# Transposing x1 by DMA instead of by TensorE, and v's product in two other banks, in a pipeline of four normalised graph layers

## The chip, the cores and the metric

The kernel runs on one core of a Trainium2 chip. The metric is the device time in microseconds (us) of one execution, taken as the median over runs.

## The reference

Eight batches (B = 8) of 1024 nodes with 128 features pass through four layers that share one 1024x1024 adjacency matrix. After each layer the result is added to its input and normalised over the features:

```python
x = _layernorm(x + _L0_gnn_ref(x, adj, ...), axis=-1)   # y = (adj @ x + x) @ w + b, rows divided by their norm
x = _layernorm(x + _L1_gnn_ref(x, adj, ...), axis=-1)   # attention, below
x = _layernorm(x + _L2_gnn_ref(x, adj, ...), axis=-1)   # (si + sj + adj * w_r + g_b) @ x @ w + b
x = _layernorm(x + _L3_gnn_ref(x, adj, ...), axis=-1)   # relu of three Chebyshev terms of the Laplacian
```

Here x1 is the result of the first line. The second layer, which the change touches, is

```python
Q = x @ q
K = x @ k
A = jnp.einsum('bnd,bmd->bnm', Q, K) / jnp.sqrt(jnp.float32(128))
A = jnp.tanh(A / 8.0) * 8.0
A = jnp.exp(A) * A_shape
A = A / jnp.sum(A, axis=-1, keepdims=True)
out = A @ x @ v
```

## The kernel before

Every float32 operand of a matrix product is split into two float16 parts, hi and lo. ScalarE (ACT in the profile) writes hi, VectorE (DVE) then writes lo as the operand minus hi, and TensorE (PE) makes each product as three matmuls (hi by hi, hi by lo, lo by hi; `split_product`, L1230 to L1234). Nodes lie in C = 8 chunks of 128 on the partitions. For a product over features x1 is needed with the features on the partitions, which is x1T.

The instructions of each engine are written out by hand in one order, with semaphores between the engines. Nothing reorders them: an instruction that waits holds up all that stand behind it on its engine. One iteration i of the loop has a `front(i)` and a `back(i)`:

- `front(i)` is the attention of batch i. For each of eight chunks t, PE makes the scores (`scores`, `next_scores`) in r1 or r0 of PSUM, ACT takes tanh and exp of them (L389, L391), DVE multiplies by the adjacency (`mask`, L846), ACT writes p_hi (L279), DVE p_lo (L851), and PE adds the chunk into av (`attend`, L1370 to L1373). Between them PE does parts of layer 2 of batch i-1 (`adj_x2_part`, `sum_x2`, `sums_w2`), whose sums DVE reads from bank m7 (`sums_read`, L738) ahead of its first mask.
- `back(i)` finishes layer 2 of batch i-1, does layer 3 of batch i-1 (`laplacian_part`, products of xq with a_hi and a_lo into r0, which DVE reads in two halves in `end_sum`, L804, semaphore `fa`), and layer 0 of batch i+1. Last it prepares the attention of batch i+1: x1 is normalised (`norm` on ACT, `ln_norm` on DVE), transposed by PE (`x1_t`, L1238, float32, eight 128x128 blocks into r1), read back and split (`x1t_hi`, `x1t_lo`), and multiplied for g (`g_product`, into r2, that is banks 0 and 1 of av) and v (`v_product`, into r1). g and v are split in turn (`g_hi`, `g_lo`, `v_hi`, `v_lo`); `v_scaled` makes a third copy of v on ACT.

The order at this seam, before: PE does `x1_t`, the second part of the first half of the last Laplacian (48 matmuls), `g_product`, `v_product`, the second part of its second half (48 matmuls), and then `scores(i+1, 0)` after a wait for `v_lo`, since r1 holds v until DVE has read it, and `scores(i+1, 1)` after a wait for `fa`, since r0 holds the Laplacian until `end_sum(i-1, 1)` has read it. DVE does the steps of `sj_step` (sums of x2 with the gate's weights) around `x1t_lo`, then `end_sum(i-1, 0)`, `g_lo`, `v_lo`, `x0_max(i+2)` (L608, absent in the last round), `end_sum(i-1, 1)`, `sj_step` 3, `sums_read`.

The sync engine (SP) issues all transfers. In the loop it loads x[i+1] when layer 0 has used x0, and stores the result of batch i-2.

```python
                x1t_lo(i + 1, r1)
                sj_step(sj_ch, i, 2)
                end_sum(i - 1, 0)
                g_lo(i + 1, r2)
                v_lo(i + 1, r1)
                if i + 2 < B:
                    x0_max(i + 2)
                end_sum(i - 1, 1)
                sj_step(sj_ch, i, 3)
```

Of the kernel before, what the change touches and what calls it, by code (L numbers as in the profile page):

```python
# [13 lines left out]
P = 128  # L14
# [62 lines left out]
def adj_resnorm(nc, x, adj, adj_t, w_first, w2, w3, rows, out):  # L77
    ctx = ExitStack()
    with ctx:
# [33 lines left out]
        x1T = sb("x1T", [P, 2, N], F16)  # L113
        xts = (x1T, sb("x1Tb", [P, 2, N], F16))
# [80 lines left out]
        def _(sp):  # L195
# [17 lines left out]
            for i in range(2, B):  # L213
                if i < B - 1:
                    sp.wait_ge(S["e0"], i + 1)
                    sp.dma_start(x0[:], x[i + 1]).then_inc(S["x_in"], 16)
                sp.wait_ge(S["ln3_a"], i - 1)
                sp.dma_start(out_v[i - 2], outb[:]).then_inc(S["stored"], 16)
# [58 lines left out]
        def _(act):  # L277
# [90 lines left out]

            def g_hi(b, src):
                for h in range(2):  # L370
                    act.wait_ge(S["g_mm"], 2 * b + h + 1)
                    copy(gs[b % 2][:, 0, half(h)], src[:, half(h)], W_DOWN).then_inc(S["g_hi"], 1)

            def v_hi(b, src):
                for h in range(2):
                    act.wait_ge(S["v_mm"], 2 * b + h + 1)
                    copy(vhis[b % 2][:, half_chunks(h), 0:D], cd(src[:])[:, half_chunks(h)], W_DOWN).then_inc(S["v_hi"], 1)
# [29 lines left out]
            def start():  # L407
# [15 lines left out]
                v_hi(0, r1)  # L423
# [11 lines left out]
                v_hi(1, r0)  # L435
# [22 lines left out]
            def back(i):  # L458
# [29 lines left out]
                x1t_hi(i + 1, r1)  # L488
                g_hi(i + 1, r2)
                v_hi(i + 1, r1)  # L490
# [44 lines left out]
        def _(dve):  # L535
# [377 lines left out]
            def start():  # L913
# [26 lines left out]
                v_lo(0, r1)  # L940
# [29 lines left out]
                v_lo(1, r0)  # L970
# [76 lines left out]
            def back(i, l2_ch):  # L1047
# [161 lines left out]
        def _(pe):  # L1209
# [167 lines left out]
            def start():  # L1377
# [14 lines left out]
                v_product(0, r1)  # L1392
# [21 lines left out]
                v_product(1, r0)  # L1414
# [33 lines left out]
            def front(i):  # L1448
# [50 lines left out]
            def back(i):  # L1499
# [133 lines left out]
```

## Time and profile before

| | |
|---|---|
| median of 3 runs | 692.7 us (691.31 to 693.2) |
| the profiled execution, its own time | 691.86 us |
| its span | 689.7 us |
| PE busy | 640.5 us, 93% |
| DVE busy | 587.4 us, 85% |
| ACT busy | 415.6 us, 60% |
| granted clock of PE, mean | 0.977 |
| hardware DMA queue, share of 16 engines | 7.7% |

The span is the profiled stretch from the first to the last instruction; the time of the same execution is 2.2 us longer. Busy time counts an engine as busy while a matmul is in its pipeline, so PE rows overlap: a 128-column matmul shows 0.22 us, and the next starts 0.056 us later. What a row of matmuls costs is therefore read from the distance of starts. The loop repeats from about 182 us to 565 us, five times, and each of these stretches takes 76.7 us.

### The profile page before, as it was taken

Reading aid. Unit: us, or ns where it says so; the run is one execution under the profiler, and the core shown is the slowest. Engines: PE = TensorE matmul, PEld = TensorE weight load, DVE = VectorE, ACT = ScalarE, POOL = GpSimd, SP = SyncE. Lnnn points to the kernel's source line nnn. Section 1 sums busy time; section 2 is a strip of 40 time slices with the busy share of each in tenths; the row PEclk is TensorE's granted clock in tenths of the full one; section 3 lists DMA queues with packets and bytes.
Section 4 is the critical chain, followed back from the end, with each engine's and each line's share of the span. In section 5 each row is a group of like instructions: output and inputs, shape, how many; then the busy total and the mean of one; then the engine's idle time right before and its main releaser. Section 6 shows DMA issues by size and latency. Waiting matters only on the chain. (4 is left out here: it accounts for less than half of the span.)

```text
span 689.7 us, 17526 instructions
## 1 busy us (share of the span) xinstructions
PE 640.5 (93%) x7435; PEld 478.3 (69%) x7435; DVE 587.4 (85%) x1521; ACT 415.6 (60%) x719; POOL 73.0 (11%) x49
## 2 busy tenths in 40 slices
PE   8897768799999999999999999999999999789895
PEld 3454536469766996669766986679666986448794
DVE  7878879688998898998998898989998889789535
ACT  6969578425692659646692649555792659323512
POOL 0102100002001100012001100021001100111002
PEclk9999988999999999999999999999999999989998
DMA  9610000000000020002000020002000000000102
GB/s 337 243 50 1 1 0 2 0 2 33 2 1 1 2 64 1 1 1 64 1 2 1 2 63 1 2 1 64 1 1 1 24 11 1 1 1 3 31 3 62
DMA packets 12446, 18.75 MB, mean 27 GB/s; under 512 B 592, under 2 KB 9040, under 8 KB 12368
## 3 DMA queue, kind: packets, MB, share of 16 engines
q1 hardware_dynamic: 12368, 17.63, 7.7%
q8 instruction: 58, 0.95, 0.6%
q14 instruction: 20, 0.16, 0.1%
HBM read 13.44 MB, written 4.19 MB: 26 GB/s over the span
## 5 line engine op out<-in xcount | busy, mean ns | idle before, releaser
L238 POOL TENSOR_TENSOR small<-small,minus_half 128x8 f32<-128x8 f32 x39 | 68.6, 1763 | 590.4 <-DVE small L572 307.1
L846 DVE TENSOR_TENSOR att<-att,adjT 128x1024 f32<-128x1024 f32 x64 | 78.0, 1219 | 11.9 <-ACT att L391 11.8
L389 ACT ACTIVATE att<-r,coef 128x1024 f32<-128x1024 f32 x64 | 70.4, 1100 | 15.1 <-PE r L1234 14.4
L851 DVE SCALAR_TENSOR_TENSOR p_lo<-p_hi,att 128x1024 f16<-128x1024 f16 x64 | 77.9, 1219 | 0.0
L1234 PE MATMUL r<-xq,a_lo 128*128 128x128 f16 x448 | 76.0, 219 | 0.0
L1232 PE MATMUL r<-xq,a_hi 128*128 128x128 f16 x448 | 76.0, 219 | 0.0
L1233 PE MATMUL r<-xq,a_hi 128*128 128x128 f16 x448 | 76.0, 219 | 0.0
L1232 PE MATMUL r<-rs,a_hi 128*128 128x128 f16 x448 | 75.8, 219 | 0.0
L1234 PE MATMUL r<-rs,a_lo 128*128 128x128 f16 x448 | 75.8, 219 | 0.0
L1233 PE MATMUL r<-rs,a_hi 128*128 128x128 f16 x448 | 75.8, 219 | 0.0
L279 ACT ACTIVATE p_hi<-att 128x1024 f16<-128x1024 f32 x64 | 66.8, 1044 | 12.7 <-DVE att L846 12.7
L391 ACT ACTIVATE att<-att 128x1024 f32<-128x1024 f32 x64 | 67.7, 1057 | 2.0
L1370 PE MATMUL av<-vhib,p_hi 128*128 128x129 f16 x256 | 46.7, 226 | 10.1 <-DVE p_lo L851 9.9
L1370 PE MATMUL av<-vhi,p_hi 128*128 128x129 f16 x256 | 45.6, 223 | 8.8 <-DVE p_lo L851 8.6
L279 ACT ACTIVATE yT<-r 128x512 f16<-128x512 f32 x16 | 9.5, 596 | 65.2 <-PE r L1234 65.1
L1373 PE MATMUL av<-vhsb,p_lo 128*128 128x129 f16 x256 | 46.8, 226 | 0.0
L1372 PE MATMUL av<-vlob,p_hi 128*128 128x128 f16 x256 | 46.7, 225 | 0.0
L1373 PE MATMUL av<-vhs,p_lo 128*128 128x129 f16 x256 | 45.7, 223 | 0.0
L1372 PE MATMUL av<-vlo,p_hi 128*128 128x128 f16 x256 | 45.6, 222 | 0.0
L1233 PEld LDWEIGHTS r<-xq,a_hi 128*128 128x128 f16 x448 | 43.7, 98 | 0.1
L1234 PEld LDWEIGHTS r<-rs,a_lo 128*128 128x128 f16 x448 | 43.8, 98 | 0.0
L1232 PEld LDWEIGHTS r<-rs,a_hi 128*128 128x128 f16 x448 | 43.7, 98 | 0.0
(383 smaller groups left out, 2104.3 us busy)
## 6 DMA issues: line engine op xcount, KB each, us to landing
adjT<-in_adj_t SPq DMA_DIRECT2D x8, 512.0 KB, 8.1
x<-in_x SPq DMA_DIRECT2D x7, 512.0 KB, 4.8
out<-outb SPq DMA_DIRECT2D x7, 512.0 KB, 3.5
pq<-in_adj SPq DMA_DIRECT2D x2, 512.0 KB, 8.7
u<-in_adj SPq DMA_DIRECT2D x2, 512.0 KB, 9.3
tmp<-in_adj SPq DMA_DIRECT2D x2, 512.0 KB, 9.8
x2s<-in_adj SPq DMA_DIRECT2D x2, 512.0 KB, 9.5
outb<-in_x SPq DMA_DIRECT2D x1, 512.0 KB, 11.6
```

Of the source, the lines that this page charges most:

```text
L238: return nc.gpsimd.tensor_tensor(dst, src, minus_half[:], ALU.pow)
L279: return nc.scalar.activation(dst, src, ACT.Copy, scale=scale, **more)
L389: nc.scalar.activation(att[:, s], dst[:], ACT.Tanh, scale=c_tanh).then_inc(S["th"], 1)
L391: nc.scalar.activation(att[:, s], att[:, s], ACT.Exp, scale=TANH_CAP).then_inc(S["ex"], 1)
L846: tt(att[:, s], att[:, s], adjT[:, t, :], ALU.mult).then_inc(S["pm"], 1)
L851: stt(p_lo[:, s], p_hi[:, s], -LO_UP, att[:, s], ALU.mult, ALU.add).then_inc(S["pl"], 1)
L1232: mm(dst, s_hi, m_hi, start=start, stop=False, skip_group_check=True)
L1233: mm(dst, s_hi, m_lo, start=False, stop=False, skip_group_check=True)
L1234: return mm(dst, s_lo, m_hi, start=False, stop=stop, skip_group_check=True)
L1370: mm(acc, p_hi[:, s, chunk(j)], vhi[:, t, 0:D + 1], start=(t == 0 and j % 3 == 0), stop=False, skip_group_check=True)
L1372: mm(acc[:, 0:D], p_hi[:, s, chunk(j)], vlo[:, t, :], start=False, stop=False, skip_group_check=True)
L1373: l_ = mm(acc, p_lo[:, s, chunk(j)], vhs[:, t, 0:D + 1], start=False, stop=(t == C - 1), skip_group_check=True)
```

## The change

Twelve transfers with transposition (two for each of the batches 2 to 7) take the place of six calls of `x1_t`. ACT and DVE split x1 as it lies in rows (`x1_row_hi`, `x1_row_lo`, both from SBUF) into a new buffer x1r, SP issues a transfer for hi when hi is written and one for lo when lo is written, and `g_product` waits for both to have landed. For batches 0 and 1 nothing changes but the way in which the banks of v are named.

On PE the first half of the last Laplacian now comes directly after the first parts, then half of what was the last block (24 matmuls), `g_product`, the other 24, and `v_product` at the very end. v goes to `av[:, 2]` and m7. `scores(i, 0)` waits for `g_lo`, and the wait for `v_lo` stands behind `scores(i, 1)`, ahead of the first write to m7. On DVE `x1_row_lo` stands ahead of the first three steps of `sj_step`.

```diff
@@ SP @@
+            for i in range(1, B - 1):
+                if i + 2 < B:
+                    sp.wait_ge(S["e0"], i + 2)
+                    sp.dma_start(x0[:], x[i + 2]).then_inc(S["x_in"], 16)
+                if i >= 2:
+                    sp.wait_ge(S["ln3_a"], i - 1)
+                    sp.dma_start(out_v[i - 2], outb[:]).then_inc(S["stored"], 16)
+                for part, name in enumerate(("hi", "lo")):
+                    sp.wait_ge(S[f"x1r_{name}"], i)
+                    sp.dma_start(cd(xts[(i + 1) % 2][:, part]), x1r[:, part], transpose=True).then_inc(S[f"x1d_{name}"], 16)
...
@@ ACT @@
+            def x1_row_hi(b):
+                act.wait_ge(S["ln0_v"], b + 1)
+                act.wait_ge(S["ln0_a"], b + 1)
+                if b > 2:
+                    act.wait_ge(S["x1d_hi"], 16 * (b - 2))
+                copy(cd(x1r[:, 0]), xas[b % 2][:], X_UP).then_inc(S["x1r_hi"], 1)
...
-                x1t_hi(i + 1, r1)
+                x1_row_hi(i + 1)
                 g_hi(i + 1, r2)
-                v_hi(i + 1, r1)
+                v_hi(i + 1, (av[:, 2], m7))
                 v_scaled(i + 1)
@@ DVE @@
+            def x1_row_lo(b):
+                if b > 2:
+                    dve.wait_ge(S["x1d_lo"], 16 * (b - 2))
+                dve.wait_ge(S["x1r_hi"], b - 1)
+                stt(cd(x1r[:, 1]), xas[b % 2][:], X_UP, cd(x1r[:, 0]), ALU.mult, ALU.subtract).then_inc(S["x1r_lo"], 1)
...
                 q_lo(z_all, i - 1, 1)
-                for k_ in range(2):
+                x1_row_lo(i + 1)
+                for k_ in range(3):
                     sj_step(sj_ch, i, k_)
-                x1t_lo(i + 1, r1)
-                sj_step(sj_ch, i, 2)
                 end_sum(i - 1, 0)
                 g_lo(i + 1, r2)
-                v_lo(i + 1, r1)
+                v_lo(i + 1, (av[:, 2], m7))
@@ PE @@
             def g_product(b, dst):
                 xt = xts[b % 2]
+                if b >= 2:
+                    pe.wait_ge(S["x1d_hi"], 16 * (b - 1))
+                    pe.wait_ge(S["x1d_lo"], 16 * (b - 1))
                 for h in range(2):
-                    pe.wait_ge(S["x1t_lo"], 2 * b + h + 1)
+                    if b < 2:
+                        pe.wait_ge(S["x1t_lo"], 2 * b + h + 1)
...
-                pe.wait_ge(S["v_lo"], 2 * (i + 1))
+                pe.wait_ge(S["g_lo"], 2 * (i + 1))
                 scores(i, 0)
                 pe.wait_ge(S["fa"], 2 * (i - 1))
                 scores(i, 1)
+                pe.wait_ge(S["v_lo"], 2 * (i + 1))
...
                 laplacian_part(r0, xq, 1, 0, C // 2)
-                x1_t(i + 1, r1)
                 pe.wait_ge(S["q_lo"], 2 * i)
                 laplacian_part(r0, xq, 0, C // 2, C).then_inc(S["o_mm"], 1)
+                laplacian_part(r0, xq, 1, C // 2, 6)
                 pe.wait_ge(S["u_ok"], i)
                 g_product(i + 1, r2)
-                v_product(i + 1, r1)
-                laplacian_part(r0, xq, 1, C // 2, C).then_inc(S["o_mm"], 1)
+                laplacian_part(r0, xq, 1, 6, C).then_inc(S["o_mm"], 1)
+                v_product(i + 1, (av[:, 2], m7))
```

How the instructions stand on DVE at the end of `back(5)`, which prepares batch 6; before:

```order
L827 TENSOR_TENSOR tmp<-xb,bias 128x1024 [waits ln1_v,ln1_a]
L829 TENSOR_REDUCE sj<-tmp 128x8 [waits sj_c]
L830 CAST one_sj<-sj 128x8 [waits sj_c]
L730 SCALAR_TENSOR_TENSOR x1T<-r,x1T 128x512 [waits x1t_hi] x2
L832 TENSOR_TENSOR tmp<-xb,bias 128x1024
L833 TENSOR_TENSOR one_sj<-sj,one_sj 128x8 [waits sj_c]
L804 SCALAR_TENSOR_TENSOR u<-r,coef,u 128x512 [waits o_mm]
L730 SCALAR_TENSOR_TENSOR g<-av,g 128x512 [waits g_hi] x2
L730 SCALAR_TENSOR_TENSOR vlo<-r,vhi 128x512 [waits v_hi] x2
L608 TENSOR_REDUCE xmax<-x 128x1 [waits x_in]
L804 SCALAR_TENSOR_TENSOR u<-r,coef,u 128x512 [waits o_mm]
```

and with the change, from the same place:

```order
L881 SCALAR_TENSOR_TENSOR x1r<-xa,x1r 128x1024 [waits x1r_hi,x1d_lo]
L844 TENSOR_TENSOR tmp<-xb,bias 128x1024 [waits ln1_v,ln1_a]
L846 TENSOR_REDUCE sj<-tmp 128x8 [waits sj_c]
L847 CAST one_sj<-sj 128x8 [waits sj_c]
L849 TENSOR_TENSOR tmp<-xb,bias 128x1024
L850 TENSOR_TENSOR one_sj<-sj,one_sj 128x8 [waits sj_c]
L821 SCALAR_TENSOR_TENSOR u<-r,coef,u 128x512 [waits o_mm]
L747 SCALAR_TENSOR_TENSOR g<-av,g 128x512 [waits g_hi] x2
L747 SCALAR_TENSOR_TENSOR vlo<-av,vhi 128x512 [waits v_hi]
L747 SCALAR_TENSOR_TENSOR vlo<-m,vhi 128x512 [waits v_hi]
L625 TENSOR_REDUCE xmax<-x 128x1 [waits x_in]
L821 SCALAR_TENSOR_TENSOR u<-r,coef,u 128x512 [waits o_mm]
```

The two halves of x1T's lo (one row, x2) have become one instruction from SBUF at the head; v_lo, x0_max (xmax) and the second end_sum (u, the last row) stand in the same order as before, behind a product that PE now makes later.

On SP, the issues of the last rounds of the loop with the change; before, only the loads of x and the stores of out stood there:

```order
L220 DMA x<-in_x 128x1024 [waits e0]
L223 DMA out<-outb 128x8x128 [waits ln3_a]
L226 DMA_TRANSPOSE x1T<-x1r 128x8x128 [waits x1r_hi]
L226 DMA_TRANSPOSE x1T<-x1r 128x8x128 [waits x1r_lo]
L223 DMA out<-outb 128x8x128 [waits ln3_a]
```

The transposing transfers stand behind the load and the store of their round, and each waits for its half of the split.

## Rows read from the trace of the kernel before

**Rows 1.** The page: its first line.
```profile
span 689.7 us, 17526 instructions
```
**Rows 2.** Busy time in one period; columns: PE, PEld, DVE, ACT, POOL, clock, DMA.
```profile
411.80:488.50 76.70, 76.66 (x928) 58.44 (x926) 69.75 (x179) 49.19 (x89) 8.23 (x5) 1.00 0.05 15
```
**Rows 3.** PE alone: x1_t, 48 Laplacian matmuls, g_product, v_product; length and busy time.
```profile
479.62:480.50 0.88, 0.88 (x11) 1.00 0.00 0
480.50:483.18 2.68, 2.68 (x50) 1.00 0.03 6
483.18:484.48 1.30, 1.30 (x10) 1.00 0.00 0
484.48:485.82 1.34, 1.34 (x26) 1.00 0.00 0
```
**Rows 4.** Timeline of DVE at the seam: start, length, line, operation, count, idle before.
```profile
475.90 1.22 DVE L841 SCALAR_TENSOR_TENSOR x2s<-xb,x2s 128x1024 f16<-128x1024 f32 x1
...
478.62 1.14 DVE L797 SCALAR_TENSOR_TENSOR xq<-pq,q_scale,xq 128x128 f16<-128x128 f32 x4
479.67 1.23 DVE L827 TENSOR_TENSOR tmp<-xb,bias 128x1024 f32<-128x1024 f32 x1
...
484.79 0.75 DVE L804 SCALAR_TENSOR_TENSOR u<-r,coef,u 128x512 f32<-128x512 f32 x1
...
486.65 1.28 DVE L730 SCALAR_TENSOR_TENSOR vlo<-r,vhi 128x512 f16<-128x512 f32 x2
487.85 1.21 DVE L608 TENSOR_REDUCE xmax<-x 128x1 f32<-128x1024 f32 x1
488.97 0.74 DVE L804 SCALAR_TENSOR_TENSOR u<-r,coef,u 128x512 f32<-128x512 f32 x1
...
491.88 0.16 DVE L738 COPY xs<-m 128x3 f32<-128x3 f32 x1 [0.77 <-PE m L1297]
...
492.60 1.22 DVE L846 TENSOR_TENSOR att<-att,adjT 128x1024 f32<-128x1024 f32 x1
```
**Rows 5.** Timeline of ACT at the seam.
```profile
477.33 1.26 ACT L322 ACTIVATE xa<-xa,small 128x128 f32<-128x128 f32 x3
...
485.35 1.27 ACT L279 ACTIVATE vhi<-r 128x512 f16<-128x512 f32 x2
...
489.99 1.11 ACT L389 ACTIVATE att<-r,coef 128x1024 f32<-128x1024 f32 x1 [2.29 <-PE r L1234]
...
492.10 1.10 ACT L389 ACTIVATE att<-r,coef 128x1024 f32<-128x1024 f32 x1
...
494.19 1.04 ACT L279 ACTIVATE p_hi<-att 128x1024 f16<-128x1024 f32 x1
```
**Rows 6.** Timeline of DVE in the front: mask 3 and p_lo 5.
```profile
500.39 1.23 DVE L846 TENSOR_TENSOR att<-att,adjT 128x1024 f32<-128x1024 f32 x1 [0.68 <-ACT att L391]
...
512.18 1.22 DVE L851 SCALAR_TENSOR_TENSOR p_lo<-p_hi,att 128x1024 f16<-128x1024 f16 x1
```
**Rows 7.** Timeline of PE there: the last filler matmul, the first of attend 5.
```profile
513.03 0.38 PE L1234 MATMUL m<-a_hi,x2s 128*128 128x512 f16 x1
513.46 0.23 PE L1370 MATMUL av<-vhi,p_hi 128*128 128x129 f16 x1
```
**Rows 8.** The last round of the seam: DVE's second end_sum.
```profile
565.41 0.75 DVE L804 SCALAR_TENSOR_TENSOR u<-r,coef,u 128x512 f32<-128x512 f32 x1 [0.77 <-PE r L1234]
```
**Rows 9.** DMA issues: transfer, count, KB each, median us from issue to landing.
```profile
x<-in_x SPq DMA_DIRECT2D x7, 512.0 KB, 4.8
out<-outb SPq DMA_DIRECT2D x7, 512.0 KB, 3.5
...
outb<-in_x SPq DMA_DIRECT2D x1, 512.0 KB, 11.6
...
out<-att SPq DMA_DIRECT2D x1, 128.0 KB, 2.7
```
**Rows 10.** Timeline of SP: the last issue of a store ahead of the seam.
```profile
472.74 0.40 SPq L218 DMA_DIRECT2D out<-outb  x1
```

More of the change, by code:

```diff
@@ L113, in adj_resnorm @@
         x1T = sb("x1T", [P, 2, N], F16)
+        x1r = sb("x1r", [P, 2, N], F16)
         xts = (x1T, sb("x1Tb", [P, 2, N], F16))
@@ L154, in cd, with chunks4 @@
             return ap.rearrange("p (c d) -> p c d", c=C)
+        def chunks4(ap):
+            return ap.rearrange("p (c d) -> p c d", d=D)
         z_all = Stage(x3, xq, rs, pq, u, outb, r0)
@@ L212, in _ @@
             sp.dma_start(x0[:], x[2]).then_inc(S["x_in"], 16)
[L213 to L218, printed above, removed]
+            for i in range(1, B - 1):
[8 more added lines that the diff above has]
+                    sp.dma_start(cd(xts[(i + 1) % 2][:, part]), x1r[:, part], transpose=True).then_inc(S[f"x1d_{name}"], 16)
+            sp.wait_ge(S["ln3_a"], B - 2)
+            sp.dma_start(out_v[B - 3], outb[:]).then_inc(S["stored"], 16)
             sp.wait_ge(S["ln3_a"], B - 1)
@@ L372, in g_hi, with v_hi @@
                     copy(gs[b % 2][:, 0, half(h)], src[:, half(h)], W_DOWN).then_inc(S["g_hi"], 1)
-            def v_hi(b, src):
+            def v_hi(b, srcs):
                 for h in range(2):
                     act.wait_ge(S["v_mm"], 2 * b + h + 1)
-                    copy(vhis[b % 2][:, half_chunks(h), 0:D], cd(src[:])[:, half_chunks(h)], W_DOWN).then_inc(S["v_hi"], 1)
+                    copy(vhis[b % 2][:, half_chunks(h), 0:D], chunks4(srcs[h][:]), W_DOWN).then_inc(S["v_hi"], 1)
             def v_scaled(b):
@@ L422, in start @@
                 y0_hi(1, 1, av[:, 2])
-                v_hi(0, r1)
+                v_hi(0, (r1[:, half(0)], r1[:, half(1)]))
                 for t in range(C):
@@ L434, in start @@
                 g_hi(1, r1)
-                v_hi(1, r0)
+                v_hi(1, (r0[:, half(0)], r0[:, half(1)]))
                 v_scaled(1)
@@ L862, in g_lo, with v_lo @@
                     split_lo(gs[b % 2][:, 1, half(h)], src[:, half(h)], W_DOWN, gs[b % 2][:, 0, half(h)], "g", 2 * b + h + 1)
-            def v_lo(b, src):
+            def v_lo(b, srcs):
                 for h in range(2):
                     hc = half_chunks(h)
-                    split_lo(vlos[b % 2][:, hc], cd(src[:])[:, hc], W_DOWN, vhis[b % 2][:, hc, 0:D], "v", 2 * b + h + 1)
+                    split_lo(vlos[b % 2][:, hc], chunks4(srcs[h][:]), W_DOWN, vhis[b % 2][:, hc, 0:D], "v", 2 * b + h + 1)
             class Rows:
@@ L939, in start @@
                 y0_lo(1, 1, av[:, 2])
-                v_lo(0, r1)
+                v_lo(0, (r1[:, half(0)], r1[:, half(1)]))
                 rows = Rows(1)
@@ L969, in start @@
                 g_lo(1, r1)
-                v_lo(1, r0)
+                v_lo(1, (r0[:, half(0)], r0[:, half(1)]))
                 row_sums(0)
@@ L1341, in g_product, with v_product @@
                 xt = xts[b % 2]
+                if b >= 2:
+                    pe.wait_ge(S["x1d_hi"], 16 * (b - 1))
+                    pe.wait_ge(S["x1d_lo"], 16 * (b - 1))
                 for h in range(2):
-                    pe.wait_ge(S["x1t_lo"], 2 * b + h + 1)
+                    if b < 2:
+                        pe.wait_ge(S["x1t_lo"], 2 * b + h + 1)
                     split_product(dst[:, half(h)], ms[:, 0], ms[:, 1], xt[:, 0, half(h)], xt[:, 1, half(h)],
                                   True, True).then_inc(S["g_mm"], 1)
-            def v_product(b, dst):
+            def v_product(b, dsts):
                 for h in range(2):
-                    project_half(dst, xts[b % 2], vs[:, 0], vs[:, 1], h).then_inc(S["v_mm"], 1)
+                    for j in range(C // 2):
+                        c = h * C // 2 + j
+                        l_ = split_product(dsts[h][:, chunk(j)], xts[b % 2][:, 0, chunk(c)], xts[b % 2][:, 1, chunk(c)],
+                                           vs[:, 0], vs[:, 1], True, True)
+                    l_.then_inc(S["v_mm"], 1)
             def scores(i, t):
@@ L1391, in start @@
                 adj_x0(1, 6, C, av[:, 2], 0)
-                v_product(0, r1)
+                v_product(0, (r1[:, half(0)], r1[:, half(1)]))
                 pe.wait_ge(S["g_lo"], 2)
@@ L1413, in start @@
                 attend(0, 7)
-                v_product(1, r0)
+                v_product(1, (r0[:, half(0)], r0[:, half(1)]))
                 pe.wait_ge(S["g_lo"], 4)
```

2 rows, old and new, of the table names are left out of this document.

## The prediction

> **What bounds the kernel now.** I read the busy shares first, then the loop by periods, then the timelines of the three engines where the change lies. The loop takes five equal periods of 76.7 us, and in one of them PE is busy 76.66 us of 76.70, DVE 69.75 and ACT 49.19 [rows 2]. So PE looks like the only bound, and a microsecond taken from PE like a microsecond won. The timelines say less. PE stands still for moments at one place of each period: the last filler matmul of the front starts at 513.03, the next matmul should follow 0.22 us later (the step between 512-column matmuls: six of them take 1.30 us [rows 3]) and starts at 513.46, 0.21 us late [rows 7]. It waits for p_lo 5 of DVE, which ends at 512.18 + 1.22 = 513.40 [rows 6]. So the chain of tanh, exp, mask and p_lo on ACT and DVE ends with PE, and what starts that chain late makes PE late.
>
> A second such place is the seam. DVE works without a gap until its second end_sum ends at 488.97 + 0.74 = 489.71 [rows 4]. PE ends its last Laplacian block, another 48 matmuls, at 484.48 + 1.34 + 2.68 = 488.50, and scores 0, six matmuls of g_product's shape, at 488.50 + 1.30 = 489.80 [rows 3]. Then come scores 1, which need that end_sum (the wait on fa): 0.09 us of slack. Behind them come sum_x2 on PE and DVE's reading of its sums at 491.88, then mask 0 at 492.60 [rows 4], and p_hi 0 on ACT at 494.19, which needs mask 0 (done at 493.82) [rows 4, 5]: 0.37 us of slack. From p_hi 0 ACT goes on without a gap, exp 3 releases mask 3 (DVE idle 0.68 us before it [rows 6]), and from mask 3 to p_lo 5 DVE has no gap. So a delay D of mask 0 reaches attend 5 as D less some 0.3 us. Three engines are balanced to a tenth of a microsecond here.
>
> **The parts, on the clock of this period.**
>
> *PE loses x1_t*: 0.88 us [rows 3], six times. It gives back a little at once: the next Laplacian part waits for q_lo, which ends at 478.62 + 1.14 = 479.76 [rows 4], so it starts at 479.82, not at 479.62. Net 0.68 us. Then 48 + 24 matmuls, 2.68 + 1.34, and PE stands before g_product at 483.84, 0.66 us later than before (483.18 [rows 3]), because of the 24.
>
> *The rows are split.* ACT's norm ends at 477.33 + 1.26 = 478.59 [rows 5] and DVE's about a tenth later, when its q_lo begins [rows 4]; hi is a copy of 128x1024 float32 to float16, like p_hi 1.04 us [rows 5], so from 478.76 to 479.80. DVE writes lo from 479.86; its nearest row is x2's lo, 1.22 us [rows 4], so until 481.08. It replaces two instructions of the same total (a pair like v_lo, 1.28 us), and DVE comes to the first end_sum at about 484.9 where it was at 484.79 [rows 4]. Price: nothing.
>
> *The transfers.* SP is free, its last store was issued at 472.74 [rows 10] and a load followed. hi goes at 479.85, lo at 481.13. No row shows a transposing transfer. Bounds from the nearest rows [rows 9]: 2.7 us (128 KB stored from SBUF) below, 11.6 us (a load among others at the start) above. In between lie 3.5 us for a store and 4.8 for a load of 512 KB, twice the size. This transfer leaves SBUF as a store does and lands in SBUF as a load does, so I take the middle, 4.15: lo lands at 485.28, and PE waits L = 485.28 - 483.84 = 1.44 us. At 2.7 us it waits 0, at 11.6 us 8.9.
> The Trainium skill, Advanced Engine Details and Errata, section X-Bar Transpose (TRN2), says that transposing transfers are as fast as plain ones, which is what taking plain rows amounts to; no row here can show it. By its page VectorE: DVE Perf Modes, section The three transpose paths, one 128x128 block takes 1309 ns; the 16 blocks of hi and lo one after another would be 20.9 us, an estimate by which L would be 16.9 us and the sum about +106 us.
>
> *v comes last.* This is the part that costs even with L = 0. g_product runs from 483.84 to 485.14 (1.30), 24 matmuls to 486.48, v to 487.82 (1.34 each). Before, v started at 484.48 and its first hi on ACT at 485.35 [rows 3, 5], 0.87 later, and both were done at 486.62. Now: first v_hi at 487.35, both done at 488.62. DVE is done with g_lo at about 486.8 (before at 486.65, where v_lo starts [rows 4]) and stands idle until v_hi; its second v_lo starts at 488.68 and, at half of the pair's distance of 1.20 us [rows 4], frees the engine at 489.28. Behind it stand x0_max (487.85 to 488.97, 1.12 us) and then the second end_sum (0.75): 490.40 to 491.15, where it was done at 489.71. The Laplacian that it reads is ready long before. Scores 1 wait on fa until 491.20, though PE is through with scores 0 at 489.12. So PE idles 2.1 us and scores 1 come 1.40 us later than before, despite the 0.68 us saved.
>
> *What follows.* sum_x2, the reading of the sums and mask 0 all move by 1.40. p_hi 0 has to wait for mask 0, done at 493.82 + 1.40 = 495.22, and starts at 495.28 where it was at 494.19: + 1.09. (tanh 1 starts at 492.7 instead of 492.10, no limit.) From there the chain without gaps carries + 1.1 us to p_lo 5 and attend 5; PE, late by 1.40, makes up 0.3 in its two small gaps. From attend 5 on PE is the bound again up to the next seam, so nothing is won back.
>
> *The sum.* Each of five periods: + 1.10 + L. In the last round (batch 7) there is no x0_max: before, its end_sum waited 0.77 us for PE [rows 8], until 565.41. Now it starts at 489.28 + 76.72 = 566.00, scores 1 at 566.80 instead of 489.80 + 76.71 = 566.51, and mask 0 0.28 later. p_hi 0 had 0.37 of slack and tanh 0 starts 0.35 earlier, so p_hi 0 comes as early as ACT allows: between 0.35 earlier and no change, and I take 0.18 earlier: - 0.18 + L. Together 5 x 1.10 - 0.18 + 6 L = 5.3 + 6 x 1.44 = + 14.0 us. Against the profiled execution's own 691.86 us (span 689.7 [rows 1]) that is 705.8; the median shown lies 0.8 above that execution, so **706.7 us**.
>
> Priced at nothing: v_scaled on ACT, now at 488.7 to 489.6, ahead of tanh 0 at 489.64 (before 489.99 [rows 5]), cover: the wait for scores; the wait for v_lo behind scores 1, over at 489.4, cover: the wait for fa; DMA traffic, 0.05 of the engines' time in a period [rows 2].
>
> **The rivals.**
>
> *Slower transposition, by blocks.* SP may hand out each of the 16 blocks as a transfer. At 0.40 us per issue [rows 10] from 479.85 the last goes at 486.25 and lands 2.7 us later [rows 9], at 488.95: L = 5.1, sum 5.3 + 30.6, 727.8 on the profiled execution, 728.6 as a median; worse if a block costs more than an issue, as the page's figure above would have it. For: nothing in this trace bounds it. Against: plain transfers of 512 KB land in 3.5 to 4.8 us.
>
> *Faster.* PE alone sets the period, and 0.68 us goes six times: - 4.1 us, 687.8, as a median 688.6. The place is the wait of scores 1 on fa; the rival holds if the second end_sum ends by 489.1, for which v_lo would have to be out of DVE two microseconds sooner than I place it, and if lo lands within 2.7 us of its issue. For it: PE's 76.66 of 76.70. Against it: the order on DVE puts v_lo and x0_max ahead of end_sum.
>
> *Nothing moves.* fa was due 0.09 us before use, so saving 0.88 us on PE wins at most 0.1 per period; if DVE comes through v_lo in time and L is 0, the time stays at 692.7.
>
> **How the numbers follow.** Forecast (1.1 us per period plus an L of 0 to 4): 0.62, own range 698 to 722. By blocks or slower: 0.22. Faster: 0.10. Nothing moves: 0.06. The first two are slower than before: 0.84. About 0.3%, 2 us, is what a measurement of this kernel can tell from no change. The range runs from 690.5, within the third case's reach, to 735, which is L = 6.1: 5.3 + 36.6 + 692.7; above it lies perhaps a third of the second case, below it the faster case.
>
> **What would show it.** Right: each period near 79.2 us; PE idle before g_product, waiting for a DMA, by 1 to 2 us, and again about 2 us before scores 1, released by DVE's L821 (end_sum); DVE idle before v_lo, released by ACT; the landing of the transposing transfers near 4 us. The two waits are separate terms: the first may be 0 and the second stays. The forecast is wrong if scores 1 follow scores 0 without a gap, or if the landing time exceeds 6 us; then the first rival's sum holds, 6 us for each microsecond of landing.

## The result, and the profile after it

| | before | after |
|---|---|---|
| median | 692.8 us (691.31 to 693.2, 4 runs) | 707.24 us (706.45 to 707.8, 4 runs) |
| ratio | | 1.0212, 95% interval 1.0198 to 1.0226 |
| profiled execution, its own time | 691.86 us | 707.8 us |
| its span | 689.7 us | 705.6 us |

The change makes the kernel 2.1% slower. The page of the changed kernel, to be held against [rows 1] and the table of before:

```profile
span 705.6 us, 17441 instructions
...
PE 636.1 (90%) x7387; PEld 473.8 (67%) x7387; DVE 589.9 (84%) x1515; ACT 416.5 (59%) x713; POOL 73.0 (10%) x49
...
x<-in_x SPq DMA_DIRECT2D x7, 512.0 KB, 3.9
out<-outb SPq DMA_DIRECT2D x7, 512.0 KB, 4.6
```

PE is busy 4.4 us less than before (640.5) and yet the span is 15.9 us longer. The work went away as meant; waits took its place. One quiet period, busy time by engine (the columns of [rows 2]):

```profile
425.23:503.55 78.32, 76.02 (x918) 57.69 (x917) 70.18 (x178) 49.37 (x89) 8.23 (x5) 1.00 0.09 22
```

PE is busy 76.02 us of 78.32, where it was 76.66 of 76.70.

**Where the 15.9 us lie.** One mark per round, DVE's first reading of sum_x2 (the copy into xs), cuts the span into stretches. "Predicted" are the prediction's terms, with its L of 1.44.

| stretch, to mark | before | after | difference | predicted |
|---|---|---|---|---|
| 1 | 128.93 | 128.12 | -0.81 | 0 |
| 2 | 56.10 | 60.92 | +4.82 | 1.40 + L = 2.84 |
| 3 | 76.72 | 79.48 | +2.76 | 1.10 + L = 2.54 |
| 4 | 76.71 | 78.34 | +1.63 | 2.54 |
| 5 | 76.71 | 78.37 | +1.66 | 2.54 |
| 6 | 76.71 | 78.32 | +1.61 | 2.54 |
| 7 | 76.57 | 80.30 | +3.73 | 0.28 + 1.10 - 1.40 + L = 1.42 |
| to the end | 121.25 | 121.75 | +0.50 | -0.18 - 0.28 = -0.46 |
| sum | 689.7 | 705.6 | +15.90 | +13.96 |

**The first wait, for the transfer.** Timeline of PE, the first matmul of g_product in each of the six rounds (called rounds 1 to 6 from here on); in brackets how long PE was idle before it, and what released it:

```profile
179.61 0.38 PE L1254 MATMUL av<-x1T,ms 128*128 128x512 f16 x1 [1.56 <-DMA x1T<-x1r]
259.09 0.38 PE L1254 MATMUL av<-x1Tb,ms 128*128 128x512 f16 x1 [1.53 <-DMA x1Tb<-x1r]
337.43 0.38 PE L1254 MATMUL av<-x1T,ms 128*128 128x512 f16 x1 [0.38 <-DMA x1T<-x1r]
415.80 0.38 PE L1254 MATMUL av<-x1Tb,ms 128*128 128x512 f16 x1 [0.42 <-DMA x1Tb<-x1r]
494.12 0.38 PE L1254 MATMUL av<-x1T,ms 128*128 128x512 f16 x1 [0.38 <-DMA x1T<-x1r]
574.05 0.38 PE L1254 MATMUL av<-x1Tb,ms 128*128 128x512 f16 x1 [1.98 <-DMA x1Tb<-x1r]
```

Idle time counts from the end of the matmul before, which is 0.16 us after the next could have started, so the starts are late by 1.72, 1.69, 0.54, 0.58, 0.53 and 2.14 us: 7.20 us in all, where the prediction had 6 x 1.44 = 8.64.

**The second wait, for fa.** The same view, first matmul of scores 1, in a quiet round and in the last:

```profile
501.45 0.39 PE L1254 MATMUL r<-g,x1T 128*128 128x512 f16 x1 [1.90 <-DVE u L821]
```
```profile
581.90 0.39 PE L1254 MATMUL r<-gb_,x1Tb 128*128 128x512 f16 x1 [0.78 <-DVE u L821]
```

It is 1.90 or 1.91 us in each of the first five rounds. The timeline of DVE at the seam shows why; it answers to [rows 4]:

```profile
489.65 1.22 DVE L881 SCALAR_TENSOR_TENSOR x1r<-xa,x1r 128x1024 f16<-128x1024 f32 x1 [0.15 <-ACT x1r L289]
...
494.71 0.75 DVE L821 SCALAR_TENSOR_TENSOR u<-r,coef,u 128x512 f32<-128x512 f32 x1
495.59 1.34 DVE L747 SCALAR_TENSOR_TENSOR g<-av,g 128x512 f16<-128x512 f32 x2
498.25 0.69 DVE L747 SCALAR_TENSOR_TENSOR vlo<-av,vhi 128x512 f16<-128x512 f32 x1 [1.32 <-ACT vhi L289]
498.92 0.69 DVE L747 SCALAR_TENSOR_TENSOR vlo<-m,vhi 128x512 f16<-128x512 f32 x1
499.53 1.21 DVE L625 TENSOR_REDUCE xmax<-x 128x1 f32<-128x1024 f32 x1
500.65 0.74 DVE L821 SCALAR_TENSOR_TENSOR u<-r,coef,u 128x512 f32<-128x512 f32 x1
...
503.55 0.16 DVE L755 COPY xs<-m 128x3 f32<-128x3 f32 x1 [0.76 <-PE m L1319]
```

Behind g_lo DVE stands 1.32 us, until v_hi is there, and the second end_sum, whose sums on PE have long been complete, waits in the queue behind v_lo and x0_max. The timeline of ACT, for [rows 5]:

```profile
488.48 1.06 ACT L289 ACTIVATE x1r<-xa 128x1024 f16<-128x1024 f32 x1
...
497.62 0.60 ACT L289 ACTIVATE vhi<-av 128x512 f16<-128x512 f32 x1 [1.41 <-PE av L1256]
...
505.53 1.06 ACT L289 ACTIVATE p_hi<-att 128x1024 f16<-128x1024 f32 x1 [0.36 <-DVE att L863]
```

**The transfers.** The transposing transfer's landing is the time from its issue until its semaphore is raised. All instances of the new issue, one row for each of the two buffers of x1T: how long an issue holds SP (minimum, median, maximum in ns), and the landing:

```profile
L226 SPq DMA_TRANSPOSE x1T<-x1r x6: 1237/1286/1322, 173.9 to 490.9; - x6
L226 SPq DMA_TRANSPOSE x1Tb<-x1r x6: 1238/1260/2383, 253.4 to 569.2; - x6
...
DMA to landing us min/median/max: 3.1/3.8/5.2
```

An issue takes 1.24 to 1.37 us (once 2.38, in round 2), three times the 0.40 us of a store [rows 10]. The page of the changed kernel, like that of the kernel before, also lists 58 transfers of 16 KB on a queue of its own, for instructions:

```profile
q8 instruction: 58, 0.95, 0.6%
```

Windows of half a microsecond (last two numbers: DMA share, GB/s): the store of the last round alone, the transposing transfers of a quiet round, and those of round 2:

```profile
562.00:562.50 0.50, 0.50 (x13) 0.50 (x11) 0.50 (x4) 0.00 (x0) 0.00 (x0) 1.00 1.04 290
...
491.00:491.50 0.50, 0.50 (x13) 0.50 (x11) 0.50 (x1) 0.00 (x0) 0.00 (x0) 1.00 1.10 213
...
255.30:255.80 0.50, 0.50 (x13) 0.50 (x11) 0.50 (x1) 0.00 (x0) 0.00 (x0) 1.00 0.72 5
```

In round 2 the transfers nearly stand still for a while. By the DMA records of the trace a 16 KB transfer of that instruction queue starts at 254.48, and transposing packets of 256 B, which take about 0.1 us in rounds 3 and 5, then take up to 1.7 us. The same is found in round 1 (from 176.73, packets of up to 1.5 us) and in the last (from 571.03, 1.5 us), and none runs while the packets of rounds 3 to 5 move. It is so in the traces of all eight kernels here that transpose by whole transfers. The last round of e3_dma_only (below) is the test that chance made: it has no such 16 KB transfer, and its last packet is done 2.8 us after lo's issue, where it takes 4.1 to 4.2 us in the last round of the other seven. So the late landings go with the loading of instructions; no run moved such a load, so that it is their cause is likely, but not isolated.

**The clock after the last wait.** Windows of the last round (columns: PE, PEld, DVE, ACT, POOL, granted clock, DMA share, GB/s):

```profile
572.00:574.05 2.05, 0.07 (x3) 0.03 (x1) 1.75 (x3) 0.00 (x0) 0.00 (x0) 1.00 0.31 65
574.05:575.80 1.75, 1.75 (x7) 0.71 (x8) 0.28 (x1) 0.60 (x1) 0.00 (x0) 0.75 0.00 0
575.80:577.50 1.70, 1.70 (x18) 1.70 (x17) 1.10 (x2) 0.60 (x1) 0.00 (x0) 0.50 0.00 0
577.50:579.00 1.50, 1.50 (x23) 1.50 (x21) 0.00 (x0) 0.00 (x0) 0.00 (x0) 0.72 0.00 0
```

PE stands 1.98 us, starts again, and its granted clock falls to 0.50, that is from 2.4 to 1.2 GHz, for some microseconds. If the work goes by the granted clock, the same windows would have done theirs at full clock in 1.75 x 0.75 + 1.70 x 0.50 + 1.50 x 0.72 = 3.24 us instead of 4.95: an estimated loss of 1.7 us, close to stretch 7's excess over its own L (3.73 - 2.14 = 1.59).

### The profile page after: what moved, and what is told of

Its sections match the earlier page's. It is cut to its first block and busy times, and to the rows that moved or that the text cites. A ratio compares the mean times of both kernels' runs of the same rounds, so it can differ in the third digit from the quotient of the medians.

```text
span 705.6 us, 17441 instructions
## 1 busy us (share of the span) xinstructions
PE 636.1 (90%) x7387; PEld 473.8 (67%) x7387; DVE 589.9 (84%) x1515; ACT 416.5 (59%) x713; POOL 73.0 (10%) x49
## 2 busy tenths in 40 slices
DMA packets 25118, 21.89 MB, mean 31 GB/s; under 512 B 13264, under 2 KB 21712, under 8 KB 25040
## 5 line engine op out<-in xcount | busy, mean ns | idle before, releaser
L1254 PE MATMUL r<-xq,a_hi 128*128 128x128 f16 x448 | 77.2, 221 | 0.1
L1255 PE MATMUL r<-xq,a_hi 128*128 128x128 f16 x448 | 77.1, 221 | 0.0
L1254 PEld LDWEIGHTS r<-xq,a_hi 128*128 128x128 f16 x448 | 44.2, 99 | 2.0 <-DVE xq L814 1.2
L1255 PEld LDWEIGHTS r<-xq,a_hi 128*128 128x128 f16 x448 | 44.2, 99 | 0.9 <-issue 0.3
L1256 PEld LDWEIGHTS r<-xq,a_lo 128*128 128x128 f16 x448 | 44.2, 99 | 0.0
```

Source lines behind the costliest of these rows:

```text
L1254: mm(dst, s_hi, m_hi, start=start, stop=False, skip_group_check=True)
L1255: mm(dst, s_hi, m_lo, start=False, stop=False, skip_group_check=True)
L1256: return mm(dst, s_lo, m_hi, start=False, stop=stop, skip_group_check=True)
```

## The experiments

A run is compared with runs of the kernel before on the same chip, whose median lay between 692.0 and 693.0 us. Theory: the time comes from two waits that do not depend on each other, the one on the transfer and the one on fa, and the second is an affair of DVE's order. Rivals: that one of the two sets the whole loss; that the transfer costs by the block.

**One half of the change alone: the order of PE, without the transfers.** `e2_order_only` keeps v at the end and in the other banks, and lets PE transpose as before. The diff shows ACT and PE; the transfers on SP and the waits for them go too, and DVE has `x1t_lo` in its old place again.

```diff
@@ changed kernel @@
-                x1_row_hi(i + 1)
+                x1t_hi(i + 1, r1)
...
+                x1_t(i + 1, r1)
...
```

> The other half of the change alone: PE transposes x1 as before, but v goes last and into the other banks. Theory A: no wait for a DMA, PE waits about 2.1 us before scores 1, each period 78.4 us, in all 9 us more than before: about 702. Theory B: as before, 691 to 694.

Measured: 702.99 us (702.18 to 703.9), ratio 1.0163, interval 1.014 to 1.0187. Quiet periods are 78.46 to 78.48 us, against 76.71 before: +1.75, which is, within 0.03, the prediction's 1.10 plus the 0.68 that PE now does not save. Scores 1 wait 1.9 us as in the changed kernel, and there is no wait for a DMA. The fa wait is an effect of the order alone.

**The other half: the transfers, with v in its old place.** `e3_dma_only`; the diff shows PE's product order, and not the banks of v and the waits for `v_lo` and `g_lo`, which are again as before.

```diff
@@ changed kernel @@
-                laplacian_part(r0, xq, 1, C // 2, 6)
                 pe.wait_ge(S["u_ok"], i)
                 g_product(i + 1, r2)
-                laplacian_part(r0, xq, 1, 6, C).then_inc(S["o_mm"], 1)
-                v_product(i + 1, (av[:, 2], m7))
+                v_product(i + 1, (r1[:, half(0)], r1[:, half(1)]))
+                laplacian_part(r0, xq, 1, C // 2, C).then_inc(S["o_mm"], 1)
...
```

> The transfers alone: x1 is split by rows and transposed by SP, but v stays in r1 and keeps its old place ahead of the last 48 Laplacian matmuls. The g product is reached 1.34 us sooner, so it waits 1.9 us in the quiet rounds and 3 to 3.5 in the rounds where the transfer landed late. Theory A: no wait before scores 1, each quiet period 1.2 us longer than before, in all about 704. Theory B gives about the same, 704; a theory by which the order alone costs gives 692.

Measured: 704.71 us (701.59 to 705.93), ratio 1.0194, interval 1.0164 to 1.0224. The waits of that kernel over two quiet periods (waiting engine and line, what it waited for, sum, times, longest):

```profile
PE av L1254 <- DMA x1Tb<-x1r: 1.8, 1, 1.8
PE av L1254 <- DMA x1T<-x1r: 1.7, 1, 1.7
```

No wait for fa is left. Quiet periods are 77.91 to 77.96, +1.22 on the mean: the wait makes g_product 1.87 us late and PE saves 0.68. In the changed kernel the 24 matmuls ahead of g_product cover 1.34 us of this wait. So v's late place does buy something, and pays more for it on DVE. Each half alone loses, and the two losses do not add: 1.75 + 1.22 would be 3.0 a period, the whole change loses 1.63.

**The fa wait taken away.** `e1_fa_first` moves one line on DVE ahead of v_lo and x0_max, `e5_max_last` the same line ahead of x0_max only:

```diff
@@ e1_fa_first, DVE, against the changed kernel @@
                 g_lo(i + 1, r2)
+                end_sum(i - 1, 1)
                 v_lo(i + 1, (av[:, 2], m7))
                 if i + 2 < B:
                     x0_max(i + 2)
-                end_sum(i - 1, 1)
@@ e5_max_last @@
                 v_lo(i + 1, (av[:, 2], m7))
+                end_sum(i - 1, 1)
                 if i + 2 < B:
                     x0_max(i + 2)
-                end_sum(i - 1, 1)
```

> The changed kernel with one DVE step moved: the second end_sum stands ahead of v_lo. Theory A (the wait of scores 1 on the second end_sum, caused by the late v_lo and x0_max ahead of it, costs 1.1 us per period on top of the transfer): that wait goes from 2.07 us to nothing, a period falls by 1.4 us in the five rounds, 707.2 goes to about 700. Theory B (only the landing of the transfers costs; the wait on end_sum takes up time that PE would lose at the attends anyway): within 2 us of 707.

> The changed kernel with only x0_max moved behind the second end_sum on DVE (v_lo stays ahead of it). The fa wait ahead of scores 1 should fall from 1.9 us to about 0.95, so that it is absorbed as in e1, quiet periods about 77.0 us (78.35 in the changed kernel). Theory A (the late second end_sum sets the round): 699 to 700. Theory B (x0_max's place is of no account, v_lo alone holds end_sum back): 706 to 707.

Measured: e1_fa_first 698.92 us (696.66 to 703.18), ratio 1.0111, interval 1.007 to 1.0153; e5_max_last 702.97 us (701.3 to 704.01), ratio 1.0142, interval 1.0116 to 1.0168. Timeline of DVE in e1_fa_first:

```profile
417.11 0.75 DVE L821 SCALAR_TENSOR_TENSOR u<-r,coef,u 128x512 f32<-128x512 f32 x1
418.41 0.69 DVE L747 SCALAR_TENSOR_TENSOR vlob<-av,vhib 128x512 f16<-128x512 f32 x1 [0.55 <-ACT vhib L289]
...
422.33 0.16 DVE L755 COPY xs<-m 128x3 f32<-128x3 f32 x1
```

and in e5_max_last:

```profile
417.65 0.69 DVE L747 SCALAR_TENSOR_TENSOR vlob<-av,vhib 128x512 f16<-128x512 f32 x1 [1.32 <-ACT vhib L289]
418.32 0.69 DVE L747 SCALAR_TENSOR_TENSOR vlob<-m,vhib 128x512 f16<-128x512 f32 x1
418.92 0.74 DVE L821 SCALAR_TENSOR_TENSOR u<-r,coef,u 128x512 f32<-128x512 f32 x1
...
422.22 0.16 DVE L755 COPY xs<-m 128x3 f32<-128x3 f32 x1
```

In e1_fa_first end_sum falls into the time in which DVE would have waited for v_hi, and costs nothing: the fa wait is gone, and quiet periods are 76.93 to 77.07. In e5_max_last the wait falls from 1.90 to 0.78 us as expected, but quiet periods are 77.55 to 77.60, not 77.0, and the time lies between the two theories. What I missed: the copy into xs has no idle time before it in the quiet rounds of either of these kernels. DVE itself sets the round there, and from the first v_lo to this copy it takes 3.92 us in the one (418.41 to 422.33) and 4.57 in the other (417.65 to 422.22). The 0.65 between is the end_sum behind v_lo. The quiet periods differ by 0.60 on the mean (77.58 and 76.98), with transfers that land 0.06 us later in e1_fa_first. So of the changed kernel's 1.4 us over e1_fa_first each round, about 0.6 is v_lo ahead of end_sum and 0.76 (78.34 less 77.58) is x0_max ahead of it. e1_fa_first, 8 us faster than the change, still loses to the kernel before: the transfer is late, and v, being last, holds DVE up.

**The transfer cut in two.** `e4_halves` issues each transfer as two, of four of its eight blocks each (the waits then count twice as many landings; not shown).

```diff
@@ changed kernel, SP @@
-                    sp.dma_start(cd(xts[(i + 1) % 2][:, part]), x1r[:, part], transpose=True).then_inc(S[f"x1d_{name}"], 16)
+                    for hh in range(2):
+                        sp.dma_start(chunks4(xts[(i + 1) % 2][:, part, half(hh)]), x1r[:, part, half(hh)],
+                                     transpose=True).then_inc(S[f"x1d_{name}"], 16)
...
```

> The changed kernel with each transposing transfer issued as two of four blocks. What it measures: an issue of eight blocks holds SP for 1.24 to 1.32 us, a plain one 0.33 to 0.40. If the issue is paid per block, each of the four takes about 0.65 us, the last lands at the same time and the kernel stays at 707. If it is a fixed price, they take 1.25 us each, the last half of lo is issued 1.3 us later, and each of the six rounds waits 1.3 us longer: 715.

Measured: 728.76 us (727.68 to 729.83), ratio 1.0521, interval 1.0481 to 1.0561. All its issues into one of the buffers, in ns, then windows of one round (columns as above):

```profile
L227 SPq DMA_TRANSPOSE x1T<-x1r x12: 1196/1267/1951, 176.1 to 509.1; - x12
```
```profile
425.00:427.40 2.40, 2.40 (x45) 2.32 (x42) 2.33 (x4) 0.00 (x0) 0.00 (x0) 1.00 0.69 80
427.40:429.90 2.50, 0.09 (x2) 0.03 (x1) 1.77 (x3) 0.00 (x0) 0.00 (x0) 0.98 0.48 94
429.90:432.50 2.60, 2.60 (x7) 0.92 (x8) 0.49 (x1) 0.60 (x1) 0.00 (x0) 0.50 0.03 6
432.50:434.00 1.50, 1.50 (x23) 1.50 (x22) 0.89 (x2) 0.60 (x1) 0.00 (x0) 0.75 0.00 0
```

Half the blocks take as long to issue: the 1.27 us are the price of an instruction. Two more issues put the last landing later, and g_product's start is late by 2.46 to 2.57 us in the quiet rounds (0.53 to 0.58 in the changed kernel). That is 1.9 to 2.0 us more, and periods grew by 3.6. The rest is the clock, at 0.50 behind this wait: 2.60 x 0.50 + 1.50 x 0.25 = 1.7 us lost. The expectation of the fixed price, 715, left the clock out and put the later landing at 1.3 us.

**The transfer covered.** Three versions put more Laplacian ahead of g_product. `v2_lap_first` does all 96 matmuls first, and DVE takes end_sum and x0_max ahead of g_lo. `v4_lap_first_relaxed` also does the 96 first, with the order end_sum, g_lo, v_lo, x0_max, and moves the fourth step of sj and the rank-one product of the loss term (`l2_rank_one`) to later places in the next front. `v5_last12_relaxed` is v4 with the last 12 matmuls behind g and v, and with g_lo, v_lo, end_sum, x0_max on DVE. In v4 and v5 one copy also goes to a buffer of its own (not shown).

```diff
@@ v4_lap_first_relaxed against the changed kernel @@
-                laplacian_part(r0, xq, 1, C // 2, 6)
+                laplacian_part(r0, xq, 1, C // 2, C).then_inc(S["o_mm"], 1)
...
-                laplacian_part(r0, xq, 1, 6, C).then_inc(S["o_mm"], 1)
...
-                    if t == 4:
+                    if t == 6:
...
+                    if t == 2:
+                        sj_step(sj_ch, i - 1, 3)
```

> The changed kernel with both causes taken away: all 96 Laplacian matmuls ahead of g and v on PE (1.34 us more cover for the transfer), and on DVE the second end_sum and x0_max ahead of g_lo and v_lo. Theory A: no wait before scores 1, a DMA wait only in the rounds that landed late (0.4 us at most), tanh 0 about 0.35 us earlier than before the change, each period 76.4 us: about 691, level with or a little under the kernel before. Theory B: the saving of 0.68 us of PE in each of six rounds counts whole: 688.7.

> All 96 Laplacian matmuls ahead of g and v, transfers by SP, and DVE relieved: the second end_sum ahead of g_lo, v_lo right after it, x0_max last, step 3 of sj moved into the front after p_lo 1 (the copy that it would meet in tmp goes to a buffer of its own), the rank-one update after p_lo 5. Theory A: PE waits 0.25 us for g_lo instead of 0.93, none for fa, and no gap at attend 4 and 5; of the 0.68 us saved 0.4 stay, with the gaps 0.75 us per period: about 688. If instead the ACT chain from v_scaled to tanh 0 (0.3 us earlier only) is the bound, about 690.

> As v4, but the last 12 Laplacian matmuls stand behind v on PE, so that g comes 0.67 us sooner, and on DVE the order is g_lo, v_lo, second end_sum, x0_max. Theory A: scores 0 need not wait for g_lo, but scores 1 wait 0.2 us for fa; in the three quiet rounds a period of about 75.9 us, in the rounds where the transfer lands late 0.5 to 1.4 us more, with a lower clock after the longest wait: 688 to 690, level with v4 or a little above.

Measured: v2_lap_first 694.17 us (692.98 to 694.88), 1.0028, interval 1.0013 to 1.0042; v4_lap_first_relaxed 693.09 (690.63 to 694.17), 0.9998, interval 0.9982 to 1.0013; v5_last12_relaxed 694.05 (692.89 to 697.39), 1.0027, interval 1.001 to 1.0043. All three recover nearly the whole loss and miss what was expected of them. In v2_lap_first I had put x0_max ahead of g_lo, and scores 0 came 0.93 us late for g_lo in the quiet rounds: periods 76.97 to 76.99. v4_lap_first_relaxed and v5_last12_relaxed have, in the quiet rounds, the periods that were expected, 75.93 to 75.94, and lost it again in the last front, which the next runs show. v5 lost more: it still waits for the transfer in rounds 1, 2 and the last (0.90, 0.62 and 1.30 us), and in its last front the granted clock falls to 0.50 for about 3 us.

**The kernel before with only the rank-one product moved.** This asks whether what v4 won came from the transposition at all. `b4_rank_later` is the kernel before with one number changed; `b6_rank_last` also moves the product behind p_lo 7 in the last front; `v6_rank_last` is v4 with the same.

```diff
@@ b6_rank_last, DVE, against the kernel before @@
-                    if t == 4:
+                    if t == 6 and nxt:
                         dve.wait_ge(S["f_c"], i - 1)
                         l2_rank_one(l2_ch, z_all, i - 1)
...
                 p_lo_part(i, C - 1)
+                if not nxt:
+                    dve.wait_ge(S["f_c"], i - 1)
+                    l2_rank_one(l2_ch, z_all, i - 1)
```

> The kernel before with one DVE step moved: the rank-one update of layer 2 (2.1 us on DVE) stands after p_lo 5 instead of after p_lo 3, so p_lo 4 and p_lo 5 come 2.1 us sooner. Theory A (the chain from tanh 0 to p_lo 5 ends together with PE): the gaps of 0.15 and 0.21 us before attend 4 and attend 5 go, five periods of 76.35 us, 1.8 us in all: 690.2 where the kernel before gives 692.0. If the chain is not a bound, no change.

> The kernel before, with the rank-one product of the loss term placed two steps later in each round and, in the last one, behind p_lo 7. From b4: quiet periods 76.33 us (76.71 before), five of them give 1.9 us. In b4 the last front lost 1.4 us, since the attend products waited 3.00 us for p_lo behind the rank product; here p_lo 6 and 7 come 2.1 us sooner, and the rank product falls into the 1.76 us in which DVE is idle ahead of the row sums. Theory A (only that order was at fault): 689 to 690 against 692.4. Theory B (the last round is bound by DVE's sum whatever the order): 692 to 693, as b4.

> The changed kernel with all 96 Laplacian products ahead of g and v (v4) and the rank product of the last round behind p_lo 7. Quiet periods 75.93 us as in v4, no wait for a transposing transfer but in the first rounds. Theory A: 688, some 2 us under b6, of which the transposition's 0.4 us a round on TensorE is what is left once the transfer is covered; theory B: equal to b6 within 0.5 us, since start and last round take it back.

| | median, us | ratio to before, interval | quiet periods, us |
|---|---|---|---|
| b4_rank_later | 692.99 | 1.0005 (0.9989 to 1.002) | 76.33 |
| b6_rank_last | 690.41 | 0.9967 (0.9954 to 0.998) | 76.33 |
| v6_rank_last | 689.65 | 0.9953 (0.9934 to 0.9972) | 75.93 |

Waits of PE for p_lo in the last front, 580 to 600 us, of the kernel before, of b4_rank_later and of b6_rank_last:

```profile
PE av L1370 <- DVE p_lo L851: 2.1, 2, 1.3
```
```profile
PE av L1370 <- DVE p_lo L851: 3.5, 2, 2.8
```
```profile
PE av L1373 <- DVE p_lo L851: 2.2, 2, 1.5
```

In b4_rank_later the product stood ahead of p_lo 6 and 7 where nothing on PE fills the time, and the wait grew by 1.4 us. Behind p_lo 7 it is free there, and both versions keep what their periods won. For b6_rank_last theory A held, to 0.4 us. For v6_rank_last it held by the periods, but the median lies between the theories, 0.76 us under b6_rank_last, and the two intervals overlap. Busy time of one quiet period, b6_rank_last and then v6_rank_last:

```profile
338.70:415.03 76.33, 76.33 (x926) 58.60 (x925) 69.86 (x178) 49.19 (x90) 8.23 (x5) 1.00 0.05 16
```
```profile
336.15:412.08 75.93, 75.83 (x917) 57.80 (x916) 70.10 (x178) 49.06 (x89) 8.23 (x5) 1.00 0.10 23
```

b6_rank_last has no gap on PE left; there TensorE is the bound, and there alone the 0.88 us of x1_t can be won. v6_rank_last differs from it in DVE's order as well, but with PE busy throughout only less work on PE can shorten the period. It wins 0.40 of the 0.88: 0.19 goes to the wait for q_lo and 0.23 to a late start of scores 0, and 0.06 I can't place. From the second mark to the end the three profiled executions take 504.67 (before), 502.45 (b6) and 501.82 us (v6): between b6 and v6 four quiet periods win 1.59 us, of which 0.63 is left, since the last stretch and the end are 0.96 us longer in v6_rank_last. Of these 0.31 lie in the last stretch, where PE waits 0.59 us for a late transfer (such waits were expected in the first rounds), and 0.38 in the landing of the very last store, 3.12 us after its issue against 2.74; the other 0.27 I can't place.

**The start.** From the first mark to the first matmul of the y2 projection the profiled executions take either 8.9 or 10.6 us and nothing between: 8.9 in the kernel before, e3, v2, v4, v5 and v6, 10.6 in the changed kernel, e1, e2, e4, e5, b4 and b6. Windows of v6_rank_last and of b6_rank_last at the same place:

```profile
130.40:134.00 3.60, 3.58 (x17) 1.68 (x18) 3.38 (x9) 0.00 (x0) 0.00 (x0) 1.00 0.00 0
```
```profile
130.40:134.00 3.60, 3.58 (x10) 1.29 (x11) 3.38 (x9) 0.00 (x0) 0.00 (x0) 0.54 0.00 0
```

It is the clock again, the 1.7 us between the two times, in a part of the program that neither change touches, behind two waits of PE (0.90 and 0.58 us) that both sorts of execution have. This is what stretch 2 of the first table has over its 1.40 + 1.72.

## Why the prediction came out right

707.24 us against 706.7 forecast, and by the mechanism that it named. The stated range, 690.5 to 735, was wide enough to be met by much else; what speaks for the mechanism is that the single terms came out. Step by step, in the quiet round around 500 us. The predicted times are shifted by 9.72 us, taken from x1_row_hi (478.76 predicted, 488.48 found), and from g_product on by another 0.53, the L of this round; the predicted times from there on are those for L = 0.

| step | predicted, shifted | found |
|---|---|---|
| x1_row_lo on DVE | 489.58 | 489.65 |
| first v_hi on ACT | 497.60 | 497.62 |
| second v_lo on DVE | 498.93 | 498.92 |
| second end_sum | 500.65 | 500.65 |
| scores 1 | 501.45 | 501.45 |
| mask 0 | 504.25 | 504.27 |
| p_hi 0 | 505.53 | 505.53 |

- **PE loses x1_t, net 0.68.** Right: the wait for q_lo costs 0.18 (0.20 predicted), and e2_order_only and e3_dma_only both need the 0.68 to come out.
- **v comes last, +1.40 at the scores, +1.10 a period.** Right within 0.05 us a period: stretches 4 to 6 less their own L are 1.09, 1.08 and 1.08. e1_fa_first and e5_max_last show that the order on DVE makes the wait, and e2_order_only that the transfer has no part in it. The prediction said that v_lo and x0_max stand in the way; their shares are about 0.6 and 0.76.
- **L = 1.44 from a landing of 4.15 us.** Near in the sum (7.20 us in six rounds against 8.64), wrong in the shape. In three rounds the lo half landed 3.1 us after its issue, and L was 0.53 to 0.58; in the three others it landed after 4.2 to 4.7 us, and L was 1.7 to 2.1. The mean of L, 1.20, came near because 4.15 happened to lie between the two groups: that is luck. None of [rows 9] told of two groups. But the page of before listed the 58 instruction transfers with which the late rounds go, and DMA traffic was priced at nothing. The rule that a transposing transfer is as fast as a plain one (the Trainium skill, Advanced Engine Details and Errata, X-Bar Transpose (TRN2)) does not hold here: while they move, the transposing transfers of a quiet round go at 163 to 213 GB/s, and the store of the last round, alone, at 290. Blocks one after another at 1309 ns each (the Trainium skill, VectorE: DVE Perf Modes, The three transpose paths) are not what happened: eight of them landed in 3.1 us.
- **The issue on SP.** Not priced: the prediction took the landing from the issue and did not ask how long an issue holds SP. It is 1.3 us in place of 0.40. That cost nothing in most rounds, since lo is written 1.3 us after hi. In round 2 lo's issue took 2.38 us, 1.1 more than in the quiet rounds, and L there is 1.1 us more than in them too. In e4_halves two more issues a round, with the clock that fell behind the longer waits, made 21.5 us.
- **The last round, -0.18 + L.** Wrong. The fa wait came as predicted: PE idle for 0.78 us and scores 1 0.94 us late, where the prediction has 0.97. But the clock fell behind the 1.98 us wait and took 1.6 us, a term that the prediction does not have, and the end is another 0.5 later where 0.46 earlier was predicted. Of that half microsecond 0.33 is the clock once more: in both kernels it stands at 0.50 behind the 5.45 us wait of PE near the end, but for 4.95 us after PE's restart with the change and for 4.29 before. Another 0.37 is the landing of the last store, 3.11 us after its issue where it was 2.74 (the 2.7 of [rows 9]); up to PE's restart the last part is 0.18 shorter. Together with the start (+0.9 net, of which 1.7 is the clock and -0.8 the first stretch) this is what the forecast lacked; the smaller L gave 1.4 of it back. The profiled execution took 707.8 us where 705.8 was forecast for it, and the median is met to 0.5 us: that owes something to terms that cancel and to the spread of the start.
- **The rivals.** By blocks: excluded by the landings of 3.1 us and by e4_halves, where four blocks take as long to issue as eight. Its own sum is 0.4 us of L too high: the last of 16 issues 0.40 us apart goes at 485.85, not 486.25. Faster: of its two conditions, e1_fa_first makes the first, v_lo out of end_sum's way, and there 0.5 to 2.1 us of waiting for the transfer remain; in the changed kernel neither holds. The gain on PE shows only where the transfer is covered and PE is the bound: quiet periods of 75.93 us in v4, v5 and v6 against 76.33 in b4 and b6, 0.4 us a round. Nothing moves: excluded by the result, whose interval begins at 1.0198.

## What to carry to other kernels

Where three engines are balanced to a tenth of a microsecond, as here, work taken from the busiest one can move the bound instead of the end: ask first which waits its instructions stood between, and take the queue of the next engine, instruction by instruction, through the new times. An instruction whose inputs are long ready must not stand behind one that waits for a product made late; one line on DVE was worth 8 of the 14 us here. And before a gain is credited to a change that came with others, give the old kernel the others alone: moving the rank-one product, with no transposition touched, gave 2.6 of the 3.4 us by which the best version beats the kernel before. Last, an average landing time can hide two kinds of rounds: look on the page for the transfers that no instruction of the kernel issues.

## What the runs showed of the hardware

- A transposing transfer from SBUF to SBUF, 128x1024 of 2 bytes, lands 3.1 to 5.2 us after its issue in the changed kernel. It holds SP for 1.24 to 1.37 us (once 2.38), and 1.2 to 1.3 us for half the size in most issues of e4_halves (up to 2.38). It moves in small packets: twelve of them raised the count of packets under 512 B from 592 to 13264, some 1056 for each transfer of 256 KB.
- It was late in 23 of the 48 rounds of eight kernels, those in which a 16 KB transfer of the instruction queue ran while its packets moved, and in no other. (One that started in its last 0.15 us, in round 5 of v5_last12_relaxed, did not count.) In the changed kernel its packets then took up to 1.5 to 1.7 us in place of 0.1. That the one makes the other is likely, but no run isolates it.
- The granted clock of TensorE fell to 0.50 after some waits in the seam and the last front, and an estimated 1.7 us was lost each time (3.4 in the last round of e4_halves). How long the wait was does not tell which: behind 1.98 us in the changed kernel's last round (and 1.99 and 1.95 us in e1 and e5 there) it fell, as behind the 2.30 to 3.48 us of e4_halves; behind 1.90 us before scores 1, and behind 2.89 and 2.27 us in e3_dma_only, it stayed at 1.00. The same wait of 2.84 us for p_lo in the last front stands in three kernels: the clock fell behind it in v5_last12_relaxed and not in b4_rank_later and v4_lap_first_relaxed. What tells them apart stays open. Behind the wait of 5.45 to 5.69 us near the end it fell in all thirteen.
- The same drop comes in the start of some executions, worth 1.7 us, and makes single executions of kernels that differ by less than that hard to compare.
